# Fused cross attention and quantised feed-forward: the centring of the second layernorm on GpSimd written as (x - mean) x 1.0 in place of (x x -1) + mean

## The reference, cut to what matters

```
x1 = x + softmax(layernorm(x) @ ctx^T / sqrt(512), masked) @ ctx
n  = layernorm(x1)
h  = gelu(silu(bitlinear(n, w1) + b1))        # 512 -> 2048
h  = layernorm(h) * g + b
out = x1 + bitlinear(h, w2) + b2              # 2048 -> 512

bitlinear(a, w): a is RMS-normalised and rounded to 8-bit steps of its
row's largest magnitude; w is rounded to -1, 0, 1 times a scale
```

## Time and profile before

| what | value |
|---|---|
| median of 3 runs | 506.21 us (505.88 to 507.05) |
| profiled execution, device time | 505.88 us |
| its span in the trace | 504.1 us |
| PE busy | 417.7 us (83%) |
| DVE busy | 450.2 us (89%) |
| ACT busy | 385.4 us (76%) |
| POOL busy | 397.1 us (79%) |
| mean granted TensorE clock | 0.915 of full speed |

### The profile page before, as it was taken

How to read it: one execution, slowest core, us unless ns; L and a number is a source line. 1 busy time by engine, 2 the same in 40 slices (tenths; PEclk the granted TensorE clock), 3 DMA queues, 4 the chain that set the end, 5 groups by cost and what they waited for, 6 DMA issues and landing times. The chain is left out here.

```text
span 504.1 us, 6676 instructions
## 1 busy us (share of the span) xinstructions
PE 417.7 (83%) x1828; PEld 195.4 (39%) x1828; DVE 450.2 (89%) x713; ACT 385.4 (76%) x492; POOL 397.1 (79%) x468
## 2 busy tenths in 40 slices
PE   0575988767989989999899989998999979892665
PEld 0452444223534544454345433544345423331222
DVE  2898699997999999999999999999999898999962
ACT  2552678897999894999698968998599987989400
POOL 0165478799898999899998999899989998884650
PEclk9988899768999997999899979999899997997769
DMA  8989450302735562574446643647253522054165
GB/s 338 384 270 342 169 166 22 126 22 83 187 79 147 154 143 67 127 218 136 104 105 190 177 116 85 175 162 166 48 141 107 125 52 59 37 105 105 43 132 138
DMA packets 93780, 69.95 MB, mean 139 GB/s; under 512 B 70312, under 2 KB 70320, under 8 KB 92976
## 3 DMA queue, kind: packets, MB, share of 16 engines
q1 hardware_dynamic: 93744, 69.52, 49.1%
HBM read 44.31 MB, written 8.39 MB: 105 GB/s over the span
## 5 line engine op out<-in xcount | busy, mean ns | idle before, releaser
L428 PE MATMUL acc<-w2q,q2T 128*128 128x512 bf16 x512 | 125.0, 397 | 21.2 <-DVE q2T L877 21.2
L415 PE MATMUL z<-w1q,q1T 128*128 128x512 bf16 x512 | 137.7, 418 | 0.0
L428 PEld LDWEIGHTS acc<-w2q,q2T 128*128 128x128 bf16 x512 | 51.9, 102 | 86.2 <-issue 36.9
L519 ACT ACTIVATE hid<-z,zs 128x1024 f32<-128x1024 f32 x64 | 70.3, 1106 | 15.4 <-PE z L415 15.2
L415 PEld LDWEIGHTS z<-w1q,q1T 128*128 128x128 bf16 x512 | 48.0, 104 | 84.3 <-issue 45.6
L857 DVE SCALAR_TENSOR_TENSOR hid<-hid,rstd,beta 128x2048 f32<-128x2048 f32 x32 | 75.3, 2353 | 2.3 <-POOL rstd L678 2.3
L848 DVE SCALAR_TENSOR_TENSOR hid<-hid,nmu,gain 128x2048 f32<-128x2048 f32 x32 | 76.3, 2385 | 0.0
L862 DVE TENSOR_REDUCE am<-hid 128x1 f32<-128x2048 f32 x32 | 72.7, 2272 | 0.0
L691 POOL TENSOR_SCALAR hid<-hid,kq 128x2048 int16<-128x2048 f32 x32 | 65.9, 2060 | 4.3 <-DVE kq L873 4.2
L539 ACT ACTIVATE junk<-hid 128x2048 bf16<-128x2048 f32 x32 | 60.9, 1904 | 5.7 <-DVE hid L857 4.8
L532 ACT ACTIVATE junk<-hid,gsum 128x2048 bf16<-128x2048 f32 x32 | 63.9, 1995 | 0.2
(11 more groups left out here) (94 smaller groups left out, 702.8 us busy)
## 6 DMA issues: line engine op xcount, KB each, us to landing
ctxT<-in_ctxT_dram SPq DMA_DIRECT2D x32, 256.0 KB, 3.6
xs<-in_x_dram SPq DMA_DIRECT2D x32, 256.0 KB, 3.5
xT<-in_xT_dram SPq DMA_DIRECT2D x32, 256.0 KB, 3.2
ctx<-in_ctx_dram SPq DMA_DIRECT2D x32, 256.0 KB, 3.1
out_dram<-xs SPq DMA_DIRECT2D x32, 256.0 KB, 2.4
hid<-in_w1T_dram SPq DMA_DIRECT2D x4, 1024.0 KB, 7.9
hid<-in_w2T_dram SPq DMA_DIRECT2D x4, 1024.0 KB, 8.7
gain<-in_g_dram SPq DMA_DIRECT2D x1, 1024.0 KB, 9.0
```

The costliest lines, as they stand in the source:

```text
L415: mm = pe.matmul(z_ps[h][:, c * CH:(c + 1) * CH], q1T[:, t % 4, k * P:(k + 1) * P], w1q[:, k, f0:f0 + CH], start=False, stop=(k == DC - 1))
L428: mm = pe.matmul(acc[t % 2][:, :], q2T[:, t % 2, c * P:(c + 1) * P], w2q[:, c, :], start=(c == 0), stop=(c == FC - 1))
L519: act.activation(hid[:, t % HR, half(h)], z_ps[h][:, :], ACT.Silu, scale=zs[:, t:t + 1]).then_inc(s_silu[h], 1)
```

## The change

The centring on POOL computes x1 minus the mean instead of the mean minus x1. Its first operation becomes a subtraction whose operand is the column of row means, its second a multiplication by the immediate 1.0; before, the first was a multiplication by the immediate -1.0 and the second an addition of the column of row means. As the centred tile now has the other sign, the factor kq1 on DVE is made with +127 instead of -127, so that the product of the two is what it was. No instruction, wait, buffer or transfer is added, removed or moved.

```diff
@@ centre_x1 (POOL)
-                pool.tensor_scalar(xc[:, t % 3, :], xs[:, t % XR, :], -1.0, mv2[:, t, 0:1],
-                                   ALU.mult, ALU.add).then_inc(s_xc, 1)
+                pool.tensor_scalar(xc[:, t % 3, :], xs[:, t % XR, :], mv2[:, t, 0:1], 1.0,
+                                   ALU.subtract, ALU.mult).then_inc(s_xc, 1)
@@ q1_scales (DVE)
-                dve.tensor_scalar(kq1[:, one], rc1[:, one], rho[:, one], -QMAX, ALU.mult, ALU.mult).then_inc(s_kq1, 1)
+                dve.tensor_scalar(kq1[:, one], rc1[:, one], rho[:, one], QMAX, ALU.mult, ALU.mult).then_inc(s_kq1, 1)
```

## The result

| | before | after |
|---|---|---|
| median of 4 runs | 506.63 us (505.88 to 507.38) | 522.08 us (520.92 to 524.15) |
| ratio, 95% interval | | 1.0321 (1.0291 to 1.0350) |
| span of the profiled execution | 504.1 us | 522.5 us |
| POOL busy | 397.1 us | 434.9 us |
| DVE busy | 450.2 us | 450.9 us |

The change makes the kernel 3.2% slower, 15.5 us by the medians. The forecast was 511.3 us: the right side, and inside the range of 505.6 to 530, but a third of the size. The profiled execution of the changed kernel is a long one: its span is 18.4 us above that of before, where the medians differ by 15.5.

A forecast was written before the change was run, and what follows sets the result against it. DVE was taken as the bound, so its waits for POOL are paid nearly in full. 11d - 1.22 = 5.14 us on the profiled 505.88 gave 511.0, plus 0.33 to the median: 511.3 us, range 505.6 to 530.

The forecast's parts named there:

- The cost of the new pair: POOL's centring L626: subtract-multiply estimated at 1.270 us, the time of L635, instead of 0.692.
- d: Extra time per centring on POOL (L626), forecast as +0.578 us.
- the bounds (0 and 1.85): Limits for the added time per centring: nothing, or two passes as slow as L635, +1.85 us.
- the rival of no change: Centring on POOL costs next to nothing more, up to 0.20 us being hidden; time stays 506.2 us; chance 0.34.
- The sum over the kappa places: DVE's L869 waits six times for POOL's kappa, delayed by centrings: 11d - 1.22, 5.14 us.
- 2d - 0.26: Kappa of tiles 6, 10, 14, 18: two centrings' delay less 0.26 us slack, about 0.9 us each.
- d - 0.18: Kappa at tile 2: one centring's delay counts, less 0.18 us slack; wait about 0.4 us.
- 1.36 + 2d: Kappa at tile 22: no slack, existing 1.36 us wait grows by both delays, to some 2.5 us.
- such meetings: Centrings on POOL running into starts of large DVE instructions, from d = 0.9 on; left out of the sum.
- The second place: rstd behind a group's other two centrings: 0.92 us slack plus 0.46 us POOL wait; costs nothing below d = 1.38.
- DVE's own instruction: L840 on DVE: only its immediate changes, 0.214 us before and after, costing nothing.

The follow-up runs named there:

- g3: New centring only in tiles 0 and 1 of each group of four, against the old kernel with plain instead of transposing transfers: 519.83 us, +15.4 us.
- h1: Old centring, one extra 360-column multiply-add (0.56 us) ahead of each, against the old kernel with plain instead of transposing transfers: 508.62 us, +3.6 us.
- g4: New centring only in tiles 2 and 3 of each group of four, against the old kernel with plain instead of transposing transfers: 505.35 us, +1.0 us.
- i2: Changed kernel with plain transfers, norm_kappa and round_q2 moved ahead of centre_x1 on POOL: 512.01 us, +7.3 us against the old kernel with plain transfers.

## Why the prediction was wrong

**The cost of the new pair** is the step that failed: "I take a single such time, 1.270 us, as my estimate", d = 0.578. It measured d = 1.31. The value lay between the bounds (0 and 1.85), but the row it was taken from was no guide: the addition of two tensors runs at (1270 - 196) / 510 = 2.1 ns per column, this pair at 3.4. With the step the rival of no change falls as well: the pair takes four times the 0.83 ns of the fast ones. The rule of the Trainium skill's GPSIMD Engine Reference (section Performance versus the Vector engine), by which up to two operations per element stay at the port's 1.03 cycles, fits three of the eight pairs tried and not the other five. The prediction called its 0.836 ns just that rate; 1.03 cycles at the page's 1.2 GHz are 0.858 ns, 3% more.

**The sum over the kappa places** held for the places. With the measured d it gives 11 x 1.31 - 1.22 = 13.2 us against 15.5 measured. Place by place: 2d - 0.26 = 2.36 by the formula, 2.43 to 2.45 measured, four times; at tile 2 d - 0.18 = 1.13 against 1.21; at tile 22 1.36 + 2d = 3.98 against 4.69. The waits for kappa grew by 16.3 - 1.4 = 14.9 us, of the 18.4 by which the profiled spans differ. g3 shows that these two centrings are the cause, and h1 that the places are right at the forecast's own delay.

**The rest** is small at d = 0.56 and some 3 us in the steady part at 1.31. Three steady groups last 358.85 - 188.60 = 170.25 us against 343.83 - 183.88 = 159.95 before: 10.3 more, of which kappa has 7.3. In the remaining 3 us DVE waits at L822 for PE (0.42 and 1.03 us, before 0.28 and 0.21), and its L877 and L857 last longer once per group (1.10 and 2.60 us, against 0.68 and 2.35), while L848 no longer takes 2.55 us once per group. The prediction left such meetings out of its sum and expected them from d = 0.9 on; the longer L877 is there in h1 already. The granted clock is also lower, 0.902 against 0.915; how much of the waits for PE hangs on it was not tried.

**The second place** (rstd, free below d = 1.38) held: g4 has the 1.31 us in just those tiles and loses 1.0 us, with an interval that takes in zero. The measured d stayed only 0.07 below that bound, so the place was not tested beyond it. DVE's other waits moved by little in the changed kernel: +2.6 for PE at L822, +1.8 for rstd, -2.7 for q2T.

**DVE's own instruction** (L840) and the rest of DVE cost nothing, as forecast: 450.9 busy us against 450.2.

What the sum does not tell is that removing the wait does not return its cost. The forecast named DVE as the bound and POOL as late at one place. That was right for small d; at 1.31 POOL has 5.2 us more per group of four tiles, and behind the kappa place a second one stood nearly as late. Of the 17.1 us, the two moves of i2 together give back some 10 by order alone. Whether the remaining 6 to 7 us are POOL's capacity beside DVE or a third meeting was not tried.

## What to carry to other kernels
On GpSimd, choose the two scalar operations of a wide instruction from the pairs that were measured to be fast, and pay with a sign carried into a later factor. A single multiplication or addition is padded with a multiplication by one, not left alone. A single subtraction is not: padded it takes 2.00 us instead of 1.57. To price a longer instruction, find where its engine leaves its last standstill and who takes a result first behind it: here two of four centrings cost nearly everything and two nearly nothing, at the same length. And when a wait is moved away by order, look at what now stands late behind it, and at what meets a large instruction of the other engine, before counting the gain.

## What was not expected of the hardware
A single multiplication of 512 columns takes GpSimd 1.57 us, a multiplication and a second one by 1.0 takes 0.70: adding an operation more than halves the time. With a subtraction it is the other way round, 1.57 alone and 2.00 with the multiplication by 1.0. Multiply-add is fast and multiply-subtract slow (0.70 against 2.01), though both are one product and one sum. Two immediates in place of a column and an immediate save 0.075 us at 512 columns (1999 against 1924). On one column the slow form costs only 0.32 us against 0.27, so small instructions do not show the difference.
